# A graph and expert kernel: the work of completed node tiles in one loop per pair of groups, and two groups per round on VectorE

## The reference

```python
deg_out = clip(segment_sum(ones, src), 1.0)
deg_in = clip(segment_sum(ones, dst), 1.0)
h = feats * rsqrt(deg_out)[:, None]
m = segment_sum(h[src], dst) * rsqrt(deg_in)[:, None]
x = m @ W_gc + b_gc + (feats @ W_res + b_res)
core = moe_ff(x)            # logits x @ Wg + bg, top 2 of 64 experts, capacity 1024 each,
                            # gelu(x @ w1 + b1) @ w2 + b2, weighted by softmax gates
y = x + core
out = layernorm(feats + batchnorm(y) * gamma + beta)
```

## Time and profile before

| | us |
|---|---|
| median of 3 runs | 3169.0 |
| lowest and highest | 3164.36, 3171.04 |
| the profiled execution | 3172.06 |
| its span, first to last instruction | 3170.3 |
| PE busy | 2126.3 (67%) |
| weight loads busy | 1746.8 (55%) |
| VectorE busy | 1250.4 (39%) |
| ScalarE busy | 395.8 (12%) |
| GpSimd busy | 2070.0 (65%) |
| mean granted clock of TensorE | 0.813 |

### The profile page before, as it was taken

How to read it: one execution, slowest core, us unless ns; L and a number is a source line. 1 busy time by engine, 2 the same in 40 slices (tenths; PEclk the granted TensorE clock), 3 DMA queues, 4 the chain that set the end, 5 groups by cost and what they waited for, 6 DMA issues and landing times.

```text
span 3170.3 us, 45195 instructions
## 1 busy us (share of the span) xinstructions
PE 2126.3 (67%) x10262; PEld 1746.8 (55%) x10263; DVE 1250.4 (39%) x3095; ACT 395.8 (12%) x1350; POOL 2070.0 (65%) x2118
## 2 busy tenths in 40 slices
PE   7955555656566665667666767777758887889360
PEld 6944444444454454545555555565547776878350
DVE  9961111122223233333444445545522122222367
ACT  1010000000000000000101111111112222222113
POOL 2017777777777777777777777777546566666703
PEclk6557767687778888888888989988969898989775
DMA  8033333333333333333333333333234454555332
GB/s 276 0 105 102 101 101 101 101 102 103 103 102 104 102 105 104 105 104 104 106 104 106 105 105 107 106 106 107 69 121 148 125 170 148 173 157 170 118 116 81
DMA packets 205309, 362.59 MB, mean 114 GB/s; under 512 B 43336, under 2 KB 126070, under 8 KB 205054
## 3 DMA queue, kind: packets, MB, share of 16 engines
q0 software_dynamic: 93888, 230.63, 25.2%
q1 hardware_dynamic: 104058, 123.31, 12.2%
q10 hardware_dynamic: 7108, 6.43, 0.6%
HBM read 328.57 MB, written 57.52 MB: 122 GB/s over the span
## 4 chain that ended last, share of the span: by engine, by line
POOL 47%; issue 22%; PE 15%; DVE 6%; DMA 4%; DVEq 2%; POOLq 2%; PEld 1%; ACT 1%; ACTq 0%; SPq 0%; PEldq 0%
POOL ring L467 21%; POOL stage L467 20%; POOL ring L494 3%; PE bank L1173 3%; PE bank L1288 3%; PE bank L1153 3%; PE bank L1282 3%; DMA ring<-nodes,slot_idx 2%; POOL y L510 2%; PE bank L1213 1%; DVE acc L1066 1%; DMA stage<-y 1%; DVE stage L775 1%; PE bank L1275 1%; PE bank L1192 1%
## 5 line engine op out<-in xcount | busy, mean ns | idle before, releaser
L467 POOL DMA_INDIRECT ring<-table,ring_idx x792 | 797.2, 1007 | 242.0 <-issue 240.7
L467 POOL DMA_INDIRECT stage<-table,ring_idx x776 | 781.1, 1007 | 236.3 <-issue 234.9
L1173 PE MATMUL bank<-ring,hot 128*128 128x257 f32 x1056 | 311.8, 459 | 187.0 <-DMA ring<-table,ring_idx 177.6
L1173 PE MATMUL bank<-stage 128*128 128x257 f32 x1040 | 306.9, 459 | 169.5 <-DMA stage<-table,ring_idx 159.6
L1173 PEld LDWEIGHTS bank<-ring,hot 128*128 128x128 f32 x1056 | 242.3, 235 | 250.7 <-issue 163.6
L1173 PEld LDWEIGHTS bank<-stage 128*128 128x128 f32 x1040 | 238.7, 235 | 232.5 <-issue 163.6
L971 DVE TENSOR_TENSOR acc<-acc,bank 128x257 f32 x196 | 82.9, 423 | 609.7 <-PE bank L1173 572.8
L510 POOL DMA_INDIRECT y<-ring,slot_idx x192 | 192.1, 1000 | 113.7 <-issue 88.9
L494 POOL DMA_INDIRECT ring<-nodes,slot_idx x192 | 198.0, 1031 | 96.5 <-POOL slot_idx L490 55.2
L1282 PEld LDWEIGHTS bank<-ring,stage 128*128 128x128 f32 x1984 | 241.9, 199 | 12.8 <-issue 6.8
L1288 PE MATMUL bank<-stage,ring 128*128 128x256 f32 x976 | 246.2, 409 | 3.3 <-ACT ring L682 3.3
(11 more groups left out here) (233 smaller groups left out, 2601.8 us busy)
## 6 DMA issues: line engine op xcount, KB each, us to landing
stage<-in_L_gnn_w_dram SPq DMA_DIRECT2D x128, 512.0 KB, 4.0
ring<-table,ring_idx POOLq DMA_INDIRECT x792
y<-zeros SPq DMA_DIRECT2D x49, 256.0 KB, 2.6
stage<-y SPq DMA_DIRECT2D x14, 896.0 KB, 7.4
stage<-table,ring_idx POOLq DMA_INDIRECT x776
stage<-in_L_gnn_b_dram SPq DMA_DIRECT2D x64, 128.0 KB
nodes<-yS ACTq DMA_DIRECT2D x49, 128.0 KB
xs<-in_x_dram SPq DMA_DIRECT2D x1, 6144.0 KB
```

The costliest lines, as they stand in the source:

```text
L467: pool.indirect_dma_start(out=ring(q)[:, j, 0:D], out_offset=None, in_=table[:, :], in_offset=bass.IndirectOffsetOnAxis(ap=ring_idx[:, q, ...
L1173: last = pe.matmul(bank[:, 0:D + 1], hots[:, j, :], ring(q)[:, j, :], start=j == 0, stop=j == CPG - 1)
```

## The change

Three things change. The check for ticks stands after every second group, and it compares the ticks before the first group of the pair with those after the second; what lies between them is run as a loop, `ticks_of_pair`. PE, ScalarE and VectorE have it alike. On VectorE the loop of the gather stage takes two groups per round, so that it runs 96 rounds, with the first pair and the last as code of their own. The other engines keep six groups per round, with three checks in it.

```diff
-        def ticks_of_group(eng, c, tick):
-            before = field(eng, c, 2)
-            now = field(eng, c, 3)
+        def ticks_of_pair(eng, pair, tick):
+            before = field(eng, group_code(eng, pair * 2), 2)
+            now = field(eng, group_code(eng, pair * 2 + 1), 3)
             with eng.If(now > before):
-                i = a_tile(before)
-
-                def behind(k, stage):
-
-                    with eng.If(i > k - 1):
...
-                tick(i, behind)
+                with eng.Fori(before, now) as t:
+                    t = a_tile(t)
+
+                    def behind(k, stage):
+                        with eng.If(t > k - 1):
...
+                    tick(t, behind)
@@ scalar
-                    ticks_of_group(act, group_code(act, it * RING + q), tick)
+                    if q % 2:
+                        ticks_of_pair(act, it * (RING // 2) + q // 2, tick)
@@ vector
-            def step(it, first, final=False):
-                for q in range(LASTQ if final else RING):
-                    g = it * RING + q
...
-                    ticks_of_group(dve, c, tick)
-            step(0, True)
-            with dve.Fori(1, STEPS - 1) as it:
-                step(it, False)
-            step(STEPS - 1, False, True)
+            def pair(p, first, final=False):
+                for h in range(2):
+                    g = p * 2 + h
+                    if not (final and h):
+                        one_hots(g + 1, 1 - h, first and h == 0)
+                    first_tile = extras(g, group_code(dve, g))
+                    dve.drain()
+                    dve.wait_ge(group_mm, g + 1)
+                    dve.tensor_tensor(acc[:, bass.ds(first_tile, 1), :], acc[:, bass.ds(first_tile, 1), :],
+                                      banks[h][:, 0:D + 1], ALU.add).then_inc(acc_added, 1)
+                ticks_of_pair(dve, p, tick)
+            pair(0, True)
+            with dve.Fori(1, GROUPS // 2 - 1) as p:
+                pair(p, False)
+            pair(GROUPS // 2 - 1, False, True)
@@ tensor
-                    ticks_of_group(pe, c, tick)
+                    if q % 2:
+                        ticks_of_pair(pe, it * (RING // 2) + q // 2, tick)
```

More of the change, by code:

```diff
@@ L299, in graph_moe_kernel @@
         DEPTH = 3
-        def ticks_of_group(eng, c, tick):
-            before = field(eng, c, 2)
-            now = field(eng, c, 3)
+        def ticks_of_pair(eng, pair, tick):
+            before = field(eng, group_code(eng, pair * 2), 2)
+            now = field(eng, group_code(eng, pair * 2 + 1), 3)
             with eng.If(now > before):
-                i = a_tile(before)
-                def behind(k, stage):
-                    with eng.If(i > k - 1):
-                        stage(nc.s_assert_within(i - k, 0, NT - 1 - k,
-                                                 skip_runtime_bounds_check_because="the branch holds it above zero"))
-                tick(i, behind)
+                with eng.Fori(before, now) as t:
+                    t = a_tile(t)
+                    def behind(k, stage):
+                        with eng.If(t > k - 1):
+                            stage(nc.s_assert_within(t - k, 0, NT - 1 - k,
+                                                     skip_runtime_bounds_check_because="the branch holds it above zero"))
+                    tick(t, behind)
         def last_ticks(eng, tick):
@@ L852, in _, with one_hots @@
             dve.reg_mov(extra, 0)
-            def one_hots(it, q, first=False):
-                g = it * RING + q
-                if not (first and q < HOTS):
-                    dve.wait_ge(group_mm, it * RING + (q - HOTS + 1))
-                dve.tensor_scalar(dstq[:, q % HOTS, :], dstT[:, bass.ds(g * CPG, CPG)], neg_base[:, bass.ds(g, 1)], None, ALU.add)
+            def one_hots(g, h, first=False):
+                if not first:
+                    dve.wait_ge(group_mm, g - 1)
+                dve.tensor_scalar(dstq[:, h, :], dstT[:, bass.ds(g * CPG, CPG)], neg_base[:, bass.ds(g, 1)], None, ALU.add)
                 dve.drain()
-                dve.tensor_tensor(hot[q % HOTS], iota_ps.unsqueeze(1).to_broadcast([P, CPG, P]),
-                                  dstq[:, q % HOTS, :].unsqueeze(2).to_broadcast([P, CPG, P]), ALU.is_equal).then_inc(hot_ready, 1)
+                dve.tensor_tensor(hot[h], iota_ps.unsqueeze(1).to_broadcast([P, CPG, P]),
+                                  dstq[:, h, :].unsqueeze(2).to_broadcast([P, CPG, P]), ALU.is_equal).then_inc(hot_ready, 1)
             def extras(g, c):
```

1 line of the change is left out of this document (removed).

## The result

The changed kernel takes 3180.7 us (median of 6 runs, 3177.3 to 3185.3), the kernel before 3169.1 us beside it. The ratio is 1.0036 with a 95% interval of 1.0023 to 1.0049: slower by 11.5 us, outside the range that was forecast (3162 to 3178). The profiled execution took 3182.57 us with a span of 3180.8, against 3172.06 and 3170.3, and its mean granted clock was 0.817 (before 0.813).

What follows compares the result with a forecast made beforehand. GpSimd's gather issue, 20.98 us a pair, was taken to bound the gather stage and hide consumers until the tail. Lag change 0 and +2.1 us in the tail, on the 3169.0 us median, gave 3171 us, range 3162 to 3178.

Steps and rivals of the forecast that it cites:

- (a): VectorE's gather loop: 30 waits of about 4 us go, 95 turns of at most 0.5 us come; hidden until the tail.
- (b): The pair check on VectorE loads two codes again between addition and tick: +1.1 us, bounds 0.6 and 1.4.
- The rival in which each turn still fetches: VectorE's round lies across a block's edge and stands 4 us at each of 95 turns: 3207 us, chance 0.05.
- (c): The loop around the tick: its end costs 0.15 us, and it runs at most once a pair.
- (d): Ticks of even groups, only before group 179, come one group later: 10 us, hidden under GpSimd's issue.
- (e): PE and ScalarE wait for VectorE's tick anyway: nothing, or at most 1 us a tick without PE's cover.
- The pace of a pair: Consumers' time for a pair of groups with a tick: 20.9 us, before 19.6.
- GpSimd's 20.98: Time in us GpSimd needs to issue the gathers of a pair of groups, whatever the other engines do.
- "I take 0 for the lag at group 193, -3 to +4": Lag, from eighth gather's end to VectorE's addition's end, taken as unchanged at group 193, bounds -3 to +4 us.
- The tail: From last gather to GpSimd's resuming: (b) counts in full before the ticks of 193 and 195, +2.1 us altogether.
- "The register work is dearer than my sum.": VectorE's loads wait for one another, the turn costs 1 us, a pair takes 21.9 us: 3177 us, chance 0.15.
- "The tail comes out early": Without stalls the lag at group 193 stays near 10.6 us in place of 17.3: 3162 us, chance 0.14.

Runs made afterwards that it cites:

- e1: The kernel before with only VectorE's loop cut from six groups a round to two, check after each group kept; 3167.3 us.
- e3: The changed kernel with VectorE and PE taking the codes from registers instead of two new loads, loop around the tick kept; 3166.0 us.
- e2: The changed kernel with VectorE and PE taking codes from registers and a plain branch instead of the loop around the tick; 3162.9 us.
- e5: e1 with two unneeded code loads on VectorE before each odd group's check, checks still per group; 3190.6 us.
- e8: e3 with two code loads put back before the check on VectorE alone; 3184.0 us.
- e12: e3 with PE's two code loads put back, VectorE's codes still from registers; 3167.3 us.
- e14: e8 with the last pair taking its codes from registers; 3181.7 us.
- e4: The changed kernel with VectorE keeping six groups a round, pair check, loads and loop around the tick kept; 3214.5 us.
- e6: e3 with one code load put back before the check on VectorE alone; 3171.3 us.
- e7: e3 with three code loads before the check on VectorE alone; 3208.4 us.
- e13: e8 with both loads moved earlier, into the even group behind its own load; 3181.5 us.
- e9: First run of e12, e3 with PE's two code loads put back, where the kernel before took 3734 us; ratio 0.9956 to it.

## Why the prediction was wrong, step by step

**(a) VectorE's loop.** Right: the stalls of 3 to 5 us are gone, the queue's packets fell from 238 to 17, and e1 shows the gain in the tail that such a loop alone brings, -8.0 us. A turn costs a bit more than forecast, 0.65 us over the 0.05 of a place inside a round, not 0.5 at most. The waits before the one-hot sum up to 131.7 us, where less than 100 was named, the longest 2.1 where none over 2 was. But that is part (b) and not the turn: behind the 49 pairs without a tick the two loads stand in front of the one-hot, with 2.0 us there against 0.9 in e3, whose sum is 76.9 us and whose longest is 1.2. The rival in which each turn still fetches falls with the 0.70 us and the 17 packets.

**(b) The loads.** The place was right, the size slightly short: the gap grew by 1.38 us, not 1.1, within the bounds given (0.6 to 1.4).

**(c), (d), (e).** The loop around the tick 0.1 us, the deferral and PE's part nothing: right, by e2 and e3, e5, e8 and e12.

**The pace of a pair.** Forecast 20.9 us, measured 20.9. GpSimd's 20.98 stood in the earlier trace rows already.

**"I take 0 for the lag at group 193, -3 to +4".** This is the step that failed. It measured +6.0. Its working started both kernels at the old kernel's 10.6 us at group 179 (10.5 when read from its rows) and asked only how the lag moves from there. But the new kernel came to group 179 with 16.1 us. Its lag was 7.7 at group 171 and 16.3 at 177: ticks stand in the pairs of 173, 175 and 177 too, at distances of 23.2 to 24.9 us, and at a pace of 20.9 nothing of that is given back. The old kernel stood at 18.0 at group 177 and was back at 10.5 two groups later, where PE even waited for the gather. The value for the start was that of a kernel which had caught up, used for one which hadn't.

The growth behind it, 6.8 before and 7.2 after, came out near the forecast (1.1 more, less 2.6 for a long stretch of products on PE), and that is in part luck: the kernels with the same two loads on VectorE grew by 7.2 (after), 9.6 (e8), 11.3 (e14) and 14.0 us (e5), and e1, e2 and e3 shrank by 2.3 to 3.0.

e1 has 13.2 us at group 179, 2.7 more than the old kernel, and is no less caught up. PE had waited longer for the gather, and the group's first 16 products took 6.41 us in place of 3.72:

```profile
2106.77 6.41 PE L1170 MATMUL bank<-stage 128*128 128x257 f32 x16 [6.77 <-DMA stage<-table,ring_idx]
```

The better sum takes e1 as the base, in which the loop is already small. Two loads a pair move its lag at 193 from 10.3 to 23.3 us. Of these 13.0, seven pairs at 1.2 us more make 8.4 and the start 2.9; the rest, 1.7, I put down to TensorE's slow stretches.

**The tail.** Forecast +2.1 us for (b) at two places. It was 1.4 at the last tick; of the tick of 193 the 1.3 is found again in the change from 193 to 195; and the forecast had no term for 1.1 us more from the last tick on. There PE began after 2.62 us idle (before 1.26), and its first products ran slower: the two at L1197 took 0.63 us where the same two (L1199) took 0.38. Four other kernels with 2.4 to 2.6 us idle there, e4, e5, e6 and e8, have this 24.3 to 24.5 us too, and the others 22.8 to 23.2, e7 among them, which idled 3.2.

**The rivals.** "The register work is dearer than my sum" was nearest in its time (3177), but not as a mechanism: it wanted a pair of 21.9, and at 20.9 it already goes this way. The point from which it decides isn't 20.98: at e13's 20.7 the lag grew by 8.9 us in seven pairs, while at e6's 20.3 it fell by 2.0. It is the room left for recovery, which must cover the long pairs, those of 22 to 24 us (before, in the mean over the seven pairs, 1.2 us a pair; after, 1.1). "The tail comes out early" was right for e1 to e3, whose tails are 29.6 to 30.0 us, and it failed here on what the prediction itself said against it: at 20.9 a pair there is no room to get early again.

**What stays open.** Three kernels lost more than the pace says, e4, e5 and e7. Spread over the seven pairs, what the long ones took over the pace is 2.0 us a pair in e5 and 2.5 in e7, where it is 1.1 in the changed kernel, so part of the bend is in them and not in the pace alone. In these three kernels more of the last 31 ticks had their first projections at 2.07 instead of 1.13 us:

| | e6 | e3 | e12 | e2 | e13 | before | after | e1 | e8 | e14 | e4 | e5 | e7 |
|---|---|---|---|---|---|---|---|---|---|---|---|---|---|
| ticks with 2.07 us, of 31 | 2 | 4 | 4 | 6 | 6 | 7 | 8 | 9 | 10 | 11 | 15 | 18 | 20 |
| PE idle before a tick, median us | 2.7 | 2.1 | 2.1 | 2.0 | 2.0 | 1.9 | 3.2 | 1.9 | 3.2 | 3.2 | 3.4 | 3.2 | 3.9 |

Where PE idles 3.2 us or more before a tick it ran 8 to 20 of them at the lower level of its clock, where it idles less 2 to 9. If the idle time is the cause, a late VectorE makes itself later still. But it is only seen side by side, e5 and the changed kernel differ in it at the same idle time, and no run here varied the one without the other.

## What to carry to other kernels

Before you ask whether an extra microsecond is hidden, set the consumer's pace beside the producer's in the densest stretch. What is left per round is the speed at which lag is given back. When it falls from 1.3 to 0.1 us, GpSimd still waits for nobody and no engine looks busier, but the whole lag comes due behind the producer's last instruction. When you carry a lag over from the old kernel, look first whether the old kernel had caught up at that point, and whether the new one can. A value that an engine has in a register is worth keeping there when its next use lies between two operations that others wait for. Where a change has two parts of opposite sign, run each alone.

## What the runs showed of the hardware that was not expected

- A load of a register took 0.30 us on VectorE and on PE, and with its register operations it put 0.5 to 0.65 us in front of VectorE's next operation, at both places where it was tried. Loads do run beside an operation in progress, but the 1.23 us one in e13 had only 0.2 us of cover left beside the work that already stood there.
- The row of the loads doesn't show that cost. In the changed kernel L285 on VectorE has 393 loads for the 197 of e12, each of the same length (least, median and longest in ns):

```profile
L285 DVEq TENSOR_LOAD <-code x393: 297/304/906, 214.7 to 2303.4; - x197
```

- A round of 599 instructions stood 3.0 to 5.0 us at its turn, one of 142 stood 0.70 behind a tick. The Trainium skill (Runtime: NRT & Kernel Launch, Instruction fetch mechanics) says that a taken branch out of the two blocks held stalls for a fetch; the packets, 238 and 17, agree. Whether a round that lies across a block's edge fetches at each turn can't be said: where VectorE's round lies isn't on record, and none of its turns shows such a stall.
- In three runs beside a kernel before of 3734.5 us, GpSimd itself waited for additions. What ended the idle time ahead of a gather, in e9 (two loads on PE alone), in us and times:

```profile
  issue: 504.6, 1489
  DVE acc L971: 425.7, 69
```

A pair with a tick then took about 30 us, and PE had idle stretches without a releaser, up to 38.4 us. The cause is not known; these runs tell nothing of the change, and their ratios are left out of the argument.
